# Sums of token rows made by GpSimd and ScalarE in place of VectorE, in a kernel of attention and mixture of experts

## What is computed

```python
def _shared_mlp(x_flat, shared_w_up_gate, shared_w_down):
    gu = jnp.einsum('td,dm->tm', x_flat, shared_w_up_gate)
    gate, up = jnp.split(gu, [J], axis=-1)
    return jnp.einsum('tm,md->td', jax.nn.silu(gate) * up, shared_w_down)

x = x + jnp.tanh(g_ffn[0]) * _L0_ffn_ref(_layernorm(x, axis=-1), ...)   # routed + shared
```

## Time and profile before

| | before |
|---|---|
| median of 3 runs | 1884.3 us (1883.9 to 1887.91) |
| the profiled execution's own time | 1901.9 us |
| its span | 1900.1 us |
| TensorE busy (matmul) | 1833.7 us, 97% |
| VectorE busy | 1163.8 us, 61% |
| ScalarE busy | 699.5 us, 37% |
| GpSimd busy | 687.8 us, 36% |
| chain that ended last | TensorE 81%, VectorE 8%, ScalarE 3%, issue 3%, GpSimd 2%, DMA 2% |

### The profile page before, as it was taken

The page is one execution under the profiler, slowest core; times in us unless marked ns, Lnnn a source line. Parts: engine busy times, 40 slices in busy tenths (PEclk is TensorE's granted clock), DMA queues, the critical chain, the costliest instruction groups (busy, mean ns, idle before and its releaser), DMA issues.

```text
span 1900.1 us, 34773 instructions
## 1 busy us (share of the span) xinstructions
PE 1833.7 (97%) x12763; PEld 1124.7 (59%) x12946; DVE 1163.8 (61%) x2294; ACT 699.5 (37%) x1978; POOL 687.8 (36%) x714
## 2 busy tenths in 40 slices
PE   7899999999999998999999999999999899999998
PEld 7565666666666564444455555555544677667675
DVE  5677777777777776475422222222236788778887
ACT  4556666666666666220122222222211111111111
POOL 3245555555555656100233343343354521010101
PEclk9999999999999999999999999999999999999999
DMA  8546666766665767513399998999943422221202
GB/s 280 153 104 134 129 136 143 143 142 147 128 144 131 167 147 163 143 48 107 84 197 236 246 219 216 222 219 209 202 135 133 121 76 80 53 90 34 78 23 89
DMA packets 478930, 268.47 MB, mean 141 GB/s; under 512 B 410704, under 2 KB 416464, under 8 KB 478800
## 3 DMA queue, kind: packets, MB, share of 16 engines
q1 hardware_dynamic: 467280, 228.90, 51.9%
q0 software_dynamic: 11520, 37.76, 7.1%
HBM read 118.72 MB, written 48.23 MB: 88 GB/s over the span
## 4 chain that ended last, share of the span: by engine, by line
PE 81%; DVE 8%; ACT 3%; issue 3%; POOL 2%; DMA 2%; another core or an unknown queue 1%; SPq 0%; DVEq 0%; ACTq 0%; POOLq 0%
PE o L637 13%; PE o L911 8%; PE score L900 7%; PE p_bank L686 7%; PE o L832 5%; PE score L783 5%; PE score L766 4%; PE p_bank L900 4%; PE m_bank L900 4%; DVE arena L1130 3%; PE m_bank L783 3%; PE t_bank L832 3%; PE p_bank L783 3%; PE c_bank L832 3%; PE p_bank L766 2%
## 5 line engine op out<-in xcount | busy, mean ns | idle before, releaser
L637 PE MATMUL o<-arena 128*128 128x512 bf16 x1474 | 339.1, 379 | 4.5 <-DVE arena L1130 1.3
L1130 DVE TENSOR_TENSOR arena<-arena 128x512 bf16<-128x512 f32 (+3 forms) x357 | 306.5, 865 | 14.4 <-ACT arena L1023 4.4
L1575 POOL TENSOR_TENSOR arena<-arena 128x512 f32<-128x512 f32 x128 | 150.7, 1178 | 304.4 <-DVE arena L1151 302.3
L988 ACT ACTIVATE arena<-score,arena 128x128 f32<-128x128 f32 x512 | 181.9, 371 | 160.4 <-DVE arena L1222 160.4
L637 PEld LDWEIGHTS o<-arena 128*128 128x128 bf16 x1536 | 147.8, 98 | 156.1 <-DVE arena L1130 1.7
L686 PE MATMUL p_bank<-arena 128*128 128x256 bf16 x1536 | 180.4, 274 | 0.8 <-DVE arena L1130 0.7
L1660 POOL TENSOR_TENSOR arena<-arena 128x1088 bf16<-128x1088 f32 x32 | 72.0, 2249 | 275.1 <-ACT arena L1013 275.1
L911 PE MATMUL o<-arena 128*128 128x512 bf16 (+1 forms) x681 | 160.0, 379 | 3.9 <-DMA arena<-arena 1.9
L686 PEld LDWEIGHTS p_bank<-arena 128*128 128x128 bf16 x1536 | 146.0, 98 | 25.4 <-DVE arena L1130 1.3
L900 PE MATMUL score<-arena 128*128 128x352 bf16 x960 | 151.5, 315 | 2.9 <-issue 2.9
L783 PE MATMUL score<-arena 128*128 128x256 bf16 x1152 | 144.0, 273 | 3.5 <-DVE arena L1505 2.2
(11 more groups left out here) (208 smaller groups left out, 3171.4 us busy)
## 6 DMA issues: line engine op xcount, KB each, us to landing
xrow_d<-arena SPq DMA_DIRECT2D x80, 256.0 KB
arena<-w_expert SPq DMA_DIRECT2D x32, 544.0 KB, 5.7
arena<-w_shared SPq DMA_DIRECT2D x22, 384.0 KB, 3.7
arena<-x SPq DMA_DIRECT2D x16, 512.0 KB, 5.0
arena<-x SPq DMA_DIRECT2D x32, 256.0 KB, 3.1
x_d<-arena SPq DMA_DIRECT2D x32, 256.0 KB, 2.6
xn_d<-arena SPq DMA_DIRECT2D x32, 256.0 KB, 2.5
arena<-x_d SPq DMA_DIRECT2D x8, 1024.0 KB
```

The source lines that it names most:

```text
L637: mm = pe.matmul(o_bank[b % 2][:, :], lhsT=cT[u % 2][:, a, h, :], rhs=M_w[:, w, head_of(hg, h), :], start=(hg == 0 and n == 0), stop=(hg = ...
L988: mm = act.activation(prob[:, u % 4, h, :], score_bank[u % 2][:, h * S:(h + 1) * S], ACT.Exp, bias=neg_max[:, u % 4, h:h + 1], accum_out=d ...
L1130: return dve.tensor_tensor(dst, src, hi, ALU.subtract)
L1575: pool.tensor_tensor(prob[:, u % 4], prob[:, u % 4], rden[:, u % 4, :].unsqueeze(2).broadcast_to([P, 4, S]), ALU.mult).then_inc(normed, 1)
```

## The change

The function `x_combine` of VectorE and its call go. GpSimd gets `x_sums_of(g, t)`, the addition and the four sums, and `x_lower(g, t)`, the lower half of the result; ScalarE copies the upper half at m = 5 and 7, behind its work of that step. In GpSimd's program the first sums stand at m = 4, the first lower half and the second sums at m = 6 behind that step's gathers, the second lower half at m = 8 behind that step's gathers. Two semaphores are added. The arithmetic is the same. The waits for the experts' last transfers, of which the buffers of the sums are a part, stood in x_combine and are made by GpSimd already, ahead of its shared steps.

```diff
@@ scalar: shared_step
+                if 22 < v < 77 and v % JT in (5, 7):
+                    t, g = v % JT // 7, v // JT + 1
+                    act.wait_ge(x_added, 5 * (2 * (g - 3) + t + 1))
+                    act.copy(combined[g % 2][:, HI, :, t, :], x_sums).then_inc(x_upper, 1)
@@ vector
-            def x_combine(g, m):
-                t = (m - 4) // 3
-                if m in (4, 7):
...
-                    rows = xs[g % 2].rearrange("p l (j t) n -> p l t j n", t=2)[:, :, t]
-                    link(dve.tensor_tensor(x32.rearrange("p j i s -> p j (i s)"), rows[:, HI], rows[:, LO], ALU.add))
-                if m in (5, 8):
-                    link(dve.tensor_tensor(x_sums[:, 0], x32[:, 0, 1], x32[:, 1, 1], ALU.add))
...
-                if m in (6, 9):
-                    link(dve.tensor_copy(combined[g % 2][:, HI, :, t, :], x_sums))
-                    lower(combined[g % 2][:, LO, :, t, :], x_sums, combined[g % 2][:, HI, :, t, :]).then_inc(x_summed, 1)
...
-                if 2 <= g < 7 and 4 <= m <= 9:
-                    x_combine(g + 1, m)
@@ gpsimd
+            def x_sums_of(g, t):
+                n = 5 * (2 * (g - 3) + t)
+
+                def link(ins, i):
+                    ins.then_inc(x_added, 1)
+                    pool.wait_ge(x_added, n + i)
+
+                pool.wait_ge(xs_in[g % 2], 64 * (g // 2 + 1))
+                rows = xs[g % 2].rearrange("p l (j t) n -> p l t j n", t=2)[:, :, t]
+                link(pool.tensor_tensor(x32.rearrange("p j i s -> p j (i s)"), rows[:, HI], rows[:, LO], ALU.add), 1)
+                link(pool.tensor_tensor(x_sums[:, 0], x32[:, 0, 1], x32[:, 1, 1], ALU.add), 2)
+                link(pool.tensor_tensor(x_sums[:, 1], x_sums[:, 0], x32[:, 0, 0], ALU.subtract), 3)
+                link(pool.tensor_tensor(x_sums[:, 2], x32[:, 0, 0], x32[:, 0, 1], ALU.subtract), 4)
+                pool.tensor_tensor(x_sums[:, 3], x32[:, 1, 0], x_sums[:, 1], ALU.subtract).then_inc(x_added, 1)
+
+            def x_lower(g, t):
+                pool.wait_ge(x_upper, 2 * (g - 3) + t + 1)
+                pool.tensor_tensor(combined[g % 2][:, LO, :, t, :], x_sums, combined[g % 2][:, HI, :, t, :],
+                                   ALU.subtract).then_inc(x_summed, 1)
+                pool.wait_ge(x_summed, 2 * (g - 3) + t + 1)
@@ gpsimd: shared_step, behind the gathers
+                if 2 <= g < 7:
+                    if m == 4:
+                        x_sums_of(g + 1, 0)
+                    if m == 6:
+                        x_lower(g + 1, 0)
+                        x_sums_of(g + 1, 1)
+                    if m == 8:
+                        x_lower(g + 1, 1)
```

More of the change, by code:

```diff
@@ L308, in build @@
         w_summed, seven_hi, seven_lo = sem("w_summed"), sem("seven_hi"), sem("seven_lo")
-        x_summed = sem("x_summed")
+        x_summed, x_added, x_upper = sem("x_summed"), sem("x_added"), sem("x_upper")
         product_mm, m1_up, half_done = sem("product_mm"), sem("m1_up"), sem("half_done")
```

## The result

| | before | after |
|---|---|---|
| median of 4 runs each, taken together | 1884.1 us (1881.07 to 1887.91) | 1905.64 us (1904.39 to 1910.35) |
| ratio to before | | 1.0117 (95%: 1.0105 to 1.013) |
| the profiled execution's own time | 1901.9 us | 1905.63 us |

The changed kernel is 1.2% slower. The forecast had the sign and 0.3% of it (1890); 1905.6 lies outside the range of 1876 to 1898. The profiled execution of after has the time of its median, that of before lay 17.8 us above its own. So the two profiles differ by 3.3 us in span and the two medians by 21.5. The kernel before has two times, near 1884 us (its runs above) or near 1897 (its first profile, at 1901.9, is of that kind); in each later set of measurements all its runs are at the same one, so what follows compares within a set only.

What follows compares the result with a forecast made beforehand. TensorE was taken as the bound, VectorE mattering only where its chain makes TensorE idle. Terms 6.2 + 3.5 + 2.1 + 2.6 - 0.5 - 8.1 = +5.8 us gave a median of about 1890, range 1876 to 1898.

Steps and rivals of the forecast that it cites:

- I expect such a pair again and carry the difference over unchanged: Whole kernel: profiled execution again 0.9% over the median, so +5.8 us makes 1901.9 into 1907.7, median about 1890.
- the term -8.1 for the "remote" wait: Slices 4 to 6, before L1505: splitting the eight gathers removes VectorE's idle time, -2.7 us three times.
- the first rival: Slices 4 to 6: VectorE's idle time before L1505 stays despite the split gathers; +13.9 us, 1898; chance 0.15.
- First sums, +6.2: Start of slices 4 to 6: GpSimd's addition and sums delay VectorE's chain, 2.05 us of TensorE each, 6.2 in all.
- Second subtraction at m = 7, +3.5: Slices 4 to 6: GpSimd's subtraction, released by ScalarE's copy, hits L1130; 1.18 us each, 3.5 in all.
- m = 6, +2.1: Slices 4 to 6: four small sums fall on the chain, 0.7 us each; the first subtraction falls between two chains.
- Slice 3, +2.6: Slice 3: +1.3 us at v=37, -1.75 at v=38, +3.1 at v=39; +2.6 in all.
- Slice 2, -0.5: v=26 to 31: gathers and load of y_sb start sooner, about half of L832's 1.13 us idle time goes; -0.5 us.
- ScalarE's copies at nothing: Ten added copies of 1024 elements cost nothing while cover lasts; otherwise the overhang, up to 1 us ten times.
- A draw: One of two large collisions misses the chain, collisions sum to 4.8 to 12.4 us; about 1884; chance 0.23.
- a faster kernel: GpSimd's instructions fall mostly beside VectorE's PSUM reads, collisions under 4.8 us; 1876 if they cost nothing; chance 0.20.

Runs made afterwards that it cites:

- the profile at the median: The kernel before, unchanged, run once more for a second profile; 1885.1 us.
- the split alone: The kernel before with its eight gathers per slice split, the last four waiting for VectorE's subtraction; 0.994 in a set with "remote" waits, 1.0002 in one without.
- the experiment that moved only the copy: The changed kernel with ScalarE's copy of the sums at m=5 and 7 moved to just after the copy of m1; 1904.16 us, 1.0098.
- the sums tied to the step: The changed kernel with GpSimd's sums, from slice 3 on, placed behind VectorE's chain, ScalarE's copies moved and the gathers between; 1888.04 us, 0.995.
- the collisions taken out by order alone: The changed kernel with GpSimd's work on row and weight sums placed behind VectorE's chain, and slice 7's gathers split too; 1877.76 us, 0.9968.
- kernel before with the weights tied: The kernel before with three added waits for GpSimd's work on the weights' sums in slice 3, nothing else; 1893.76 us, 0.999.
- a memset: The changed kernel with GpSimd's twelve instructions per slice for the sums replaced by memsets of the same regions, waits kept; 1882.08 us, 0.9986.
- with everything tied: The changed kernel with GpSimd's row sums placed behind VectorE's chain and its weights' sums in slice 3 made to wait too; 1882.62 us, 0.993.

## Why the prediction was wrong, point by point

**Its base.** The step that failed is "I expect such a pair again and carry the difference over unchanged", together with the term -8.1 for the "remote" wait. Of the surplus of 17.8 us of the profiled execution over the median, 8.5 us are these very waits in slices 4 to 6 (slice 4 takes 81.8 us in the earlier trace rows and 78.9 in the profile at the median), and 2.1 more are those of slice 7. An execution at the median has no such wait, so no change could take it away there. With that term at zero the forecast's own sum is +13.9, or 1898, which stood in it as the first rival for another reason: the stall doesn't stay, it was never in the median. As a mechanism the term was right: the split alone is 0.994 where the stalls exist. The median lies 7.6 us beyond even that, for which the terms mis-sized below stand.

That the forecast for the profiled execution, 1907.7, comes within 2.1 us of the measured 1905.63 is luck: the whole surplus of 16.8 us went where 8.1 were forecast to go, and the collisions and slice 2 came to 20.2 where 13.9 were forecast.

**First sums, +6.2, measured 8.7.** A mis-sized term, though mechanism and place held: the addition began 0.57 us before the multiply and held it to 0.5 us beyond its own end. Two of the slices lost 2.05 and 2.5 us, the third 4.1, of which about 1.6 are the clock's fall, which was in no term.

**Second subtraction at m = 7, +3.5, measured 3.4.** Right, and for the reason given: 2.50 us beside 2.36, as in the earlier trace rows, and the experiment that moved only the copy took back 1.13 us a slice.

**m = 6, +2.1, measured 5.2.** The term that was mis-sized most. The forecast put the second sums on the chain and let the first subtraction fall between two chains. The lines of after show the subtraction on the chain: L1134 begins at 1609.22 and takes 3.08 us, to 0.55 us beyond the end of a subtraction that begins only at 1609.62, 0.02 us behind the fourth gather. Here the order of the recorded starts doesn't say who waits, though the prediction had gone by it. L1134 began 0.40 us before GpSimd's subtraction (0.38 in slices 5 and 6) and lost in all three slices; with the sums tied to the step, where ScalarE's copy releases GpSimd's subtraction, L1139 begins 0.40 us before it too and keeps its 0.69. A gather alone doesn't hold it: with the sums tied, L1139 at 1606.22 keeps 0.69 us beside one from 1605.63 to 1606.58. Why the instruction directly behind a gather wins isn't shown; the price is a whole instruction of 2 us. The step takes 8.90 us for 6.83; 0.35 of the difference come back, since VectorE's own addition no longer delays the step before (7.17 for 7.52), and 1.7 us a slice are left, three times.

**Slice 3, +2.6, measured 2.7** in the pair of profiles (0.22 to 2.93 us apart). The pieces are those named: at v = 37 +0.8 us (forecast +1.3), at v = 38 -1.1 (-1.75), at v = 39 +2.8 (+3.1), where subtraction and addition stand in a row against the chain.

**Slice 2, -0.5, measured +0.2** at the start of slice 3, which is less than profiles of one kernel differ there (1483.50 and 1481.94 in two of after). **ScalarE's copies at nothing** held but in one place. At v = 38 the copy L1124 and the one for the weights (L1090) stand in a row before ScalarE's next copy out of PSUM (L1110), and TensorE idles 0.54 us for that one; the forecast had named this overhang. It is the most of what v = 38 lacks of its -1.75.

**The whole.** 8.7 + 5.2 + 3.4 + 2.7 + 0.2 = 20.2 us, the difference of the two profiles near their medians at slice 7, against 21.5 in the medians. Of the 7.6 us between 1898 and the 1905.6 measured, 3.1 are m = 6, 2.5 the first sums, 0.7 slice 2, and the rest is the scatter of medians. The experiments confirm it from the other side: with the collisions taken out by order alone, the same work on the same engines makes a kernel faster than before (0.9968).

**The rivals.** A draw and a faster kernel asked for collisions of under 12.4 and 4.8 us; they were 20. Both came out of doubt in a reading of the earlier trace rows that all runs bear out. The 0.43 given to these two was too much, since the rows had shown the exclusion already; it is also what pulled the range down to 1876, while its upper end, the stall's 1898, left no room for larger collisions on top of that.

**What stays open.** What makes a set of measurements one with or without the "remote" waits, at the same program on the same chip. The density of the transfers doesn't tell the two apart: in the step v = 49 of the kernel before, from 0.61 to 4.61 us after its multiply, they move 316 GB/s in a profile with the wait (the one at 1897.6 us) and 321 in one without (at 1885.1):

```profile
1602.65:1606.65 4.00, 3.95 (x27) 2.57 (x27) 3.69 (x10) 0.42 (x1) 3.09 (x4) 1.00 0.93 316
```

```profile
1604.00:1608.00 4.00, 4.00 (x28) 2.56 (x27) 3.69 (x10) 0.42 (x1) 3.09 (x4) 1.00 0.91 321
```

Splitting the gathers removes the wait, but it also puts the last four of them later, so that closeness and place are not told apart by it. By what path eight in a row hold up VectorE isn't shown.

## What to carry to other kernels

Before arithmetic goes to GpSimd, lay each of its instructions over VectorE's chain in time: a GpSimd instruction that reads SBUF cost VectorE's two-input instructions and casts up to about its own whole length wherever they met, and where it starts (a wait on the chain's last semaphore) is worth more than how much is moved. Where the start of such an instruction is known only to a few tenths of a microsecond, count the collision as likely, at full price, also where the records would put VectorE's instruction first. And when the profiled execution is slower than the median, find what the surplus consists of before any term of the sum is taken from it.

## What the hardware showed that was not expected

**The clock can fall after one wait of about two microseconds.** TensorE's granted clock fell to its lower level (1.2 of 2.4 GHz) after a single long wait in the midst of full work. Windows of after around 1743, with 2.25 us of idle time in the first:

```profile
1738.00:1743.20 5.20, 3.01 (x28) 2.44 (x25) 4.91 (x6) 0.68 (x2) 4.42 (x4) 1.00 0.01 3
1743.20:1745.80 2.60, 2.54 (x7) 0.90 (x8) 2.40 (x6) 0.42 (x1) 1.31 (x2) 0.52 0.00 0
```

The step takes 10.76 us, while the same collision in slice 4 takes 8.71. In the second profile of after it happens at four such places (v = 39, 44, 55 and 66), with steps of 10.6 to 11.6 us; where the first profile kept the full clock, these steps are 1.7 to 1.9 us longer than there. It doesn't follow each such gap: after idles of 2.35 us (v = 55) and 2.52 (v = 39) in the first profile it stayed full. The shortest idle time that it followed in the profiles read here was 1.97 us (kernel before with the weights tied, v = 49), and the same kernel kept the full clock after 1.96 (v = 60) and 2.08 (v = 71). So the same collision at v = 44 cost 2.1 us in one execution (8.71 for 6.65) and 4.0 in another (10.61).

**A copy of fp32 to bf16 is held up too, and by mere writes as well.** The cast L1518, 0.43 us alone, takes 0.83 us beside a GpSimd sum and 2.23 at v = 39 (profile of after), where GpSimd's addition starts before it. The forecast had used this much. New is that a memset holds it also (1.26 us beside 0.95, above), where the multiply and the subtraction keep their 0.69:

```profile
1532.91 2.46 POOL L1706 TENSOR_TENSOR arena<-arena 128x1024 f32<-128x1024 bf16 x1
1533.42 2.23 DVE L1518 CAST arena<-arena 128x512 bf16<-128x512 f32 x1
```

**GpSimd against VectorE, same form:** addition of 1024 elements 2.12 against 1.27 us, subtraction 2.14 against 1.23, sum of 256 elements 0.72 against 0.43, all undisturbed: a ratio of 1.7. The ten halves cost GpSimd 71 us (759.0 for 687.8 with everything tied) for VectorE's 42 without the casts, and both engines had the time; only the place was at fault.
